# Attention takes its query tiles in the order middle, last, first, and the block's products stand ahead of the exponentials

## The reference

```python
h = tok(x)                       # gray, two 3x3 Scharr convolutions, (|dx| + |dy|) / 2: 256 rows of 256
h = concat([h, text(x_txt)])     # 128 rows of a low-rank embedding: 384 rows of 256 per image
h = h + attention(layernorm(h))  # 16 heads of 16, query i sees keys i-128 .. i
h = h + routed(layernorm(h))     # the 288 rows with the highest score get gelu(x @ w_block), the others x
h = h + ssm(layernorm(h))        # linear recurrence with a circulant matrix, done in the Fourier basis
h = h + moe(layernorm(h))        # shared FFN of 1024 plus two of eight experts, gated
```

## Time and profile before

| | us |
|---|---|
| median of three runs | 2317.09 (2313.73 to 2319.89) |
| profiled execution, its own time | 2323.64 |
| its span | 2321.8 |
| images 2 to 14, each, from one copy of `hc` to the next | 95.6 |
| image 0, with all loads | 158.6 |

### The profile page before, as it was taken

The page is one execution under the profiler, slowest core; times in us unless marked ns, Lnnn a source line. Parts: engine busy times, 40 slices in busy tenths (PEclk is TensorE's granted clock), DMA queues, the critical chain, the costliest instruction groups (busy, mean ns, idle before and its releaser), DMA issues.

```text
span 2321.8 us, 45095 instructions
## 1 busy us (share of the span) xinstructions
PE 2038.4 (88%) x13718; PEld 1599.1 (69%) x13812; DVE 1320.7 (57%) x3533; ACT 1111.4 (48%) x2541; POOL 796.0 (34%) x1535
## 2 busy tenths in 40 slices
PE   3778898898988989989899898987589999999997
PEld 1455666566665666666666566654489999999997
DVE  4536566565665666656566565664255555555554
ACT  0335445545455544554545545552155445655543
POOL 2213223232333323233322333233244544444454
PEclk9789999999999999999999999998789999999999
DMA  4210211202112021020220211201133223333222
GB/s 129 63 41 15 62 43 34 61 7 61 47 28 61 15 60 44 24 61 24 50 51 18 61 31 44 48 8 55 61 107 79 45 45 79 78 51 79 48 45 41
DMA packets 83556, 116.35 MB, mean 50 GB/s; under 512 B 23718, under 2 KB 63974, under 8 KB 81190
## 3 DMA queue, kind: packets, MB, share of 16 engines
q1 hardware_dynamic: 57414, 85.14, 13.7%
q0 software_dynamic: 23360, 27.91, 7.3%
q10 hardware_dynamic: 2736, 2.76, 0.4%
HBM read 51.58 MB, written 26.71 MB: 34 GB/s over the span
## 4 chain that ended last, share of the span: by engine, by line
PE 57%; issue 15%; DVE 13%; POOL 5%; ACT 4%; DMA 3%; SPq 1%; DVEq 1%; POOLq 0%; ACTq 0%
PE ps L1743 9%; PE ps L1598 6%; PE ps L1517 4%; PE ps L1463 3%; PE ps L1755 3%; PE ps L1756 3%; PE ps L1754 3%; PE ps L1585 3%; PE ps L1530 2%; PE ps L1508 2%; PE ps L1635 2%; DMA result<-yb,idx_o 2%; PE ps L1437 2%; PE ps L1485 2%; ACT prob L781 2%
## 5 line engine op out<-in xcount | busy, mean ns | idle before, releaser
L1092 DVE TENSOR_REDUCE mx<-ps 128x2 f32<-128x512 f32 (+1 forms) x384 | 227.8, 597 | 298.7 <-PE ps L1509 250.1
L781 ACT ACTIVATE prob<-ps,mx 128x256 f32<-128x256 f32 (+1 forms) x768 | 295.4, 445 | 165.5 <-DVE mx L1092 146.0
L773 ACT ACTIVATE pT<-ps 128x512 f32<-128x512 f32 (+1 forms) x384 | 204.0, 531 | 337.4 <-PE ps L1517 336.8
L883 ACT ACTIVATE hid_hi<-ps,b 128x256 fp32r<-128x256 f32 x408 | 204.5, 501 | 287.9 <-PE ps L1743 287.4
L1508 PE MATMUL ps<-ks,qs 96*128 96x512 f32 (+1 forms) x384 | 198.5, 522 | 71.6 <-issue 36.3
L1368 DVE TENSOR_TENSOR hid_lo<-hid_full,hid_hi 128x256 fp32r<-128x256 f32 x408 | 171.8, 426 | 151.8 <-ACT hid_full L886 140.6
L1517 PE MATMUL ps<-ident,prob 128*128 128x128 f32 x1280 | 211.4, 281 | 27.7 <-ACT prob L781 21.7
L1754 PE MATMUL ps<-w_hi,hid_hi 128*128 128x256 f32 x816 | 233.9, 287 | 0.0
L1755 PE MATMUL ps<-w_lo,hid_hi 128*128 128x256 f32 x816 | 229.6, 281 | 0.0
L1756 PE MATMUL ps<-w_hi,hid_lo 128*128 128x256 f32 x816 | 229.6, 281 | 0.0
L886 ACT ACTIVATE hid_full<-ps,b 128x256 f32<-128x256 f32 x408 | 205.1, 503 | 0.3 <-DVE hid_lo L1368 0.3
(11 more groups left out here) (256 smaller groups left out, 4311.6 us busy)
## 6 DMA issues: line engine op xcount, KB each, us to landing
w_raw<-in_w SPq DMA_DIRECT2D x16, 1024.0 KB, 6.0
xin<-in_x SPq DMA_DIRECT2D x32, 384.0 KB, 3.8
qs<-q_hi SPq DMA_DIRECT2D x128, 96.0 KB
ks<-k_hi SPq DMA_DIRECT2D x256, 48.0 KB
qs<-q_lo SPq DMA_DIRECT2D x64, 96.0 KB
ks<-k_lo SPq DMA_DIRECT2D x128, 48.0 KB
xn_rows<-xc SPq DMA_DIRECT2D x16, 384.0 KB, 2.5
result<-h SPq DMA_DIRECT2D x16, 384.0 KB, 2.5
```

Source lines behind the costliest of these rows:

```text
L781: ins = act.activation(prob[:, s % PB, hh, w], ps[:, s % 2, hh * 2 * P + w.start:(hh + 1) * 2 * P], ACT.Exp, bias=mx[:, s % 2, hh:hh + 1])
L883: act.activation(hid_hi[:, f], ps[:, f % 4, 0:CHUNK], ACT.Gelu_apprx_tanh, bias=b1[half][:, f:f + 1])
L1092: dve.tensor_reduce(mx[:, s % 2], sc, AX_X, ALU.max, negate=True).then_inc(max_done.sem, 1)
```

## The change

`ORDER = (1, 2, 0)`: units 0 to 7 are now those of the middle query tile, 8 to 15 of the last, 16 to 23 of the first, and each place that asked for the tile by the slot asks `ORDER`. The output projections move to slots `WO` = 16, 24, 31 (15, 23, 31 before). The slot constants move: the first `turn_chain` to slot 1; router scores and all three block tiles to slot 2, ahead of unit 2; on ScalarE the copies of `xcT` and `srow` and the block's Gelu to slot 0, ahead of the first exponential; rank counts to slots 1 to 3; `slot_ranks` to slot 1, now into PSUM bank 4, with a wait of TensorE for `cnt_ready` in slot 4; the sum over the values to slot 2; the `down` steps to slots 2, 3, 4, 5, 7, 8; text to 3 and 5; gray to 11; the second `turn_chain` to 12, the recurrence to 14, the edge steps to 15 to 18, `state_out` and `make_rows` to 19. The logits on VectorE move from slots 28 to 30 to slots 30 to 32, the `up` steps to slots 30 and 31 (one each) and behind the last slot (six). The value product no longer waits for the low part of the queries, and for its third tile waits for VectorE's last read of the keys' bank (`k_read`). No arithmetic is added or taken away.

```diff
@@ -42,17 +42,20 @@
 UPT = NH // HG
+ORDER = (1, 2, 0)
 PB, TB = 3, 3
...
 VW = 2 * DK
-
-RANKS, TURN0, BLOCK, RANK = 4, 2, 4, 6
-DOWN, TEXT, GRAY_AT, TURN1 = 8, 8, 13, 15
-STATE, CONV, OUT = 17, 18, 22
-ROWS, TURN2, UP = 22, 27, 28
-UPS = {29: (0, 1, 2), 31: (3,), 32: (4,)}
-UPS_LAST = (5, 6, 7)
+WO = [UPT * (i + 1) + PV + 4 + (i < NT - 1) for i in range(NT)]
+
+RANKS, TURN0, BLOCK, RANK = 1, 1, 2, 1
+TEXT, GRAY_AT, TURN1 = 3, 11, 12
+DOWNS = {2: 0, 3: 1, 4: 2, 5: 3, 7: 4, 8: 5}
+STATE, CONV, OUT = 14, 15, 19
+ROWS, TURN2, UP, LOGIT = 19, 27, 28, 30
+UPS = {30: (0,), 31: (1,)}
+UPS_LAST = (2, 3, 4, 5, 6, 7)
 NEWTON = 3
@@ -767,14 +771,14 @@
                     u = s - TURN
-                    k0 = 0 if u >= UPT else 1
+                    k0 = 0 if ORDER[u // UPT] else 1
                     act.wait_ge(turned.sem, turned.at(b, u + 1))
...
                 if s < NU:
-                    w = slice(0 if s >= UPT else P, 2 * P)
+                    w = slice(0 if ORDER[s // UPT] else P, 2 * P)
                     act.wait_ge(max_done.sem, max_done.at(b, s + 1))
@@ -835,17 +839,19 @@
                     if chain:
-                        if s in (TURN0, TURN1):
-                            turned_rows(b - 1, (TURN0, TURN1).index(s))
-                        if s in (BLOCK + 1, BLOCK + 2):
-                            block_outputs(b - 1, s - BLOCK - 1)
+                        if s == 0:
+                            turned_rows(b - 1, 0)
+                            block_outputs(b - 1, 0)
+                            block_outputs(b - 1, 1)
+                        if s == TURN1:
+                            turned_rows(b - 1, 1)
                     if att:
...
                         round_first()
-                    if head and s == TEXT - 1:
+                    if head and s == TEXT - 2:
                         text_rows(b + 1)
@@ -1062,8 +1068,9 @@
                 for m in range(KB):
-                    dve.scalar_tensor_tensor(out=k_lo[:, m], in0=ps[:, 2 + m, 0:T], scalar=bk[:, m:m + 1],
-                                             in1=k_hi[:, m], op0=ALU.add, op1=ALU.subtract)
+                    ins = dve.scalar_tensor_tensor(out=k_lo[:, m], in0=ps[:, 2 + m, 0:T], scalar=bk[:, m:m + 1],
+                                                   in1=k_hi[:, m], op0=ALU.add, op1=ALU.subtract)
+                ins.then_inc(k_read.sem, 1)
@@ -1103,11 +1110,11 @@
                     dve.tensor_tensor(cx[:], cx[:], sumv[:], ALU.add).then_inc(cx_ready.sem, 1)
-                if s >= UPT + PV + 5 and (s - UPT - PV - 5) % UPT == 0:
-                    i = (s - UPT - PV - 5) // UPT
+                if s - 1 in WO:
+                    i = WO.index(s - 1)
                     dve.wait_ge(wo_done.sem, wo_done.at(b, i + 1))
                     dve.wait_ge(hbo_ready.sem, hbo_ready.at(b, 1))
-                    dve.tensor_tensor(h1[:, i], hbo[:, i], ps[:, 5, D:2 * D], ALU.add).then_inc(h1_ready.sem, 1)
+                    dve.tensor_tensor(h1[:, ORDER[i]], hbo[:, ORDER[i]], ps[:, 5, D:2 * D], ALU.add).then_inc(h1_ready.sem, 1)
@@ -1199,7 +1206,7 @@
                     chain_scale(b, 2)
-                if s == UP:
+                if s == LOGIT:
@@ -1210,14 +1217,14 @@
                     link(ins, chain_step, b)
-                if s == UP + 1:
+                if s == LOGIT + 1:
                     dve.memset(spare[:], 0.0)
...
                     link(dve.tensor_copy(pick[:], i8[:, :, 0:2].rearrange("p i k -> p k i")), chain_step, b)
-                if s == UP + 2:
+                if s == LOGIT + 2:
                     link(dve.tensor_tensor(hot[:].rearrange("p k i e -> p (k i) e"),
@@ -1240,7 +1247,7 @@
                 link(dve.tensor_tensor(picked[:], hot[:].rearrange("p k i e -> p k (i e)"),
-                                       ps[:, 5, 0:NT * NE].unsqueeze(1).to_broadcast([P, 2, NT * NE]), ALU.mult),
+                                       ps[:, 4, 0:NT * NE].unsqueeze(1).to_broadcast([P, 2, NT * NE]), ALU.mult),
                      slot_step, b)
@@ -1277,7 +1284,7 @@
                         powers(2 ** (s - 2))
-                    if late and s == DOWN + 6:
+                    if late and s == max(DOWNS) + 1:
                         shared_sum(b - 2)
@@ -1478,8 +1485,9 @@
                 pe.wait_ge(ctx_ready.sem, ctx_ready.at(b, 0))
-                pe.wait_ge(parts_ready.sem, parts_ready.at(b, 1))
                 for i in range(NT):
+                    if i == 2:
+                        pe.wait_ge(k_read.sem, k_read.at(b, 1))
                     dst = ps[:, 4, i * D:(i + 1) * D] if i < 2 else ps[:, 3, 0:D]
@@ -1496,12 +1504,12 @@
                 if s < NU:
-                    i, g = s // UPT, s % UPT
+                    i, g = ORDER[s // UPT], s % UPT
                     c0 = 0 if i else P
...
                     m, r = g % KB, g // KB
-                    if i == 0 and m == 0:
+                    if s < UPT and m == 0:
                         pe.wait_ge(stacked[r].sem, stacked[r].at(b, stacked[r].per))
@@ -1513,15 +1521,15 @@
                     for hh in range(HG):
-                        for k in range(0 if u >= UPT else 1, 2):
+                        for k in range(0 if ORDER[u // UPT] else 1, 2):
                             ins = pe.transpose(ps[:, 2 + u % 2, (2 * hh + k) * P:(2 * hh + k + 1) * P],
...
                     u = s - PV
-                    i, g = u // UPT, u % UPT
+                    i, g = ORDER[u // UPT], u % UPT
                     if g == 1:
-                        pe.wait_ge(ctx_ready.sem, ctx_ready.at(b, i))
+                        pe.wait_ge(ctx_ready.sem, ctx_ready.at(b, u // UPT))
                     pe.wait_ge(pT_ready.sem, pT_ready.at(b, u + 1))
@@ -1544,8 +1552,8 @@
                     ins.then_inc(cx_turned.sem, 1)
-                if s >= UPT + PV + 4 and (s - UPT - PV - 4) % UPT == 0:
-                    i = (s - UPT - PV - 4) // UPT
+                if s in WO:
+                    i = WO.index(s)
                     pe.wait_ge(cxT_ready.sem, cxT_ready.at(b, i + 1))
@@ -1605,27 +1613,27 @@
                 if att:
-                    pe.wait_ge(sumv_ready.sem, sumv_ready.at(b + 2, 1))
+                    pe.wait_ge(v_ready.sem, v_ready.at(b + 2, 1))
                 flat_hot = hot2[:].rearrange("p i e -> p (i e)")
                 w = NT * NE
-                pe.matmul(ps[:, 5, 0:w], ltri[:], flat_hot, start=True, stop=False)
+                pe.matmul(ps[:, 4, 0:w], ltri[:], flat_hot, start=True, stop=False)
                 for i in range(1, NT):
-                    pe.matmul(ps[:, 5, i * NE:w], ones_bf[:], flat_hot[:, 0:w - i * NE], start=False, stop=False)
-                pe.matmul(ps[:, 5, 0:w].rearrange("p (i e) -> p i e", i=NT), ones_bf[:],
+                    pe.matmul(ps[:, 4, i * NE:w], ones_bf[:], flat_hot[:, 0:w - i * NE], start=False, stop=False)
+                pe.matmul(ps[:, 4, 0:w].rearrange("p (i e) -> p i e", i=NT), ones_bf[:],
                           cnt[:].unsqueeze(1).to_broadcast([P, NT, NE]), start=False, stop=True
...
             def chain(b, s, head):
-                if s in (TURN0, TURN1, TURN2):
+                if s in (TURN1, TURN2):
                     turn_chain(b, (TURN0, TURN1, TURN2).index(s), head)
...
                     for k in range(KB):
-                        pe.matmul(ps[:, 7, 0:T], wr_bc[:, k], xcT[:, k], start=(k == 0), stop=(k == KB - 1))
+                        ins = pe.matmul(ps[:, 7, 0:T], wr_bc[:, k], xcT[:, k], start=(k == 0), stop=(k == KB - 1))
+                    ins.then_inc(block_done.sem, 1)
                     block_tile(0)
-                    block_tile(1).then_inc(block_done.sem, 1)
-                if s == BLOCK + 2:
+                    block_tile(1)
                     pe.wait_ge(block_ready.sem, block_ready.at(b, 1))
@@ -1663,18 +1671,24 @@
                         values(b + 1)
+                    if att and s == BLOCK:
+                        values_sum(b)
+                    if late and s == BLOCK:
+                        down(b - 2, 0, chained, head)
+                    if late and s == PV + 1:
+                        pe.wait_ge(cnt_ready.sem, cnt_ready.at(b - 2, 1))
+                    if chained and s == TURN0:
+                        turn_chain(b - 1, 0, head)
                     if att:
                         unit(b, s)
-                    if att and s == 1:
-                        values_sum(b)
                     if late and s == RANKS:
...
                         text(b + 1)
-                    if late and DOWN <= s < DOWN + 6:
-                        down(b - 2, s - DOWN, chained, head)
+                    if late and s > BLOCK and s in DOWNS:
+                        down(b - 2, DOWNS[s], chained, head)
                     if head and CONV <= s < CONV + 4:
...
                     if chained and s == OUT:
```

(1 more changed line is left out.)

## The result

| | us |
|---|---|
| median of four runs after the change | 2228.89 (2226.42 to 2231.07) |
| the kernel before, four runs beside it | 2318.49 (2313.73 to 2322.36) |
| ratio | 0.9614, 95% interval 0.9591 to 0.9637 |
| profiled execution after, its own time and its span | 2226.72 and 2224.9 |
| images 2 to 14, mean, from one copy of `hc` to the next | 89.8 (95.6 before) |

What follows compares the result with a forecast made beforehand. TensorE, busy 88%, bounds the kernel through its waits. Minus 67.6 us for images 2 to 14 and minus 7 elsewhere take 2323.6 to 2249.0; less 6.5 for the runs' median, 2242.5 us, range 2212 to 2284.

Steps and rivals of the forecast that it cites:

- What bounds the kernel, and the work itself: Whole image: TensorE's work without the slow clock about 85.3 us; its waits go from 8.9 to 5.1.
- Front: Slots 0 to 2: two of four table loads go, four waits become 0.3 us, minus 4.1 an image.
- The clock: TensorE's slow stretch beside the 2.52 us wait: with that wait gone, 0.9 us an image is taken back.
- Middle: Slots 3 to 14: nothing waits, and the 1.57 us wait before the second `turn_chain` goes.
- Last tile: Slots 16 to 26: half-size units cover handoffs less; waits of 4.3 us, the largest 1.75; plus 2.3 an image.
- End: Last residual to the next `turn_chain`: 0.55 us open where 0.88 was, minus 0.3 an image.
- Images 0, 1 and 15, and behind: Three images outside 2 to 14: minus 3 us each; pass behind the last image: plus 2; together minus 7.
- The series of the last tile: Rival: from slot 20 each unit takes a full round, 11.2 us more per image, 2388 in all; chance 0.06.
- Half the gain goes back: Rival: five waits each 0.5 us longer, or the clock falls there; images of 92 to 94, 2263 to 2289; chance 0.17.
- Near TensorE's work alone: Rival: the last tile costs less than counted; images of 87 to 88.5 us, time 2198 to 2218; chance 0.13.
- The table load: ScalarE's table switches: 1.28 us per load, with no drain in the trace where the skill gives another 1.38.

Runs made afterwards that it cites:

- the natural order: The changed kernel with the query tiles in the order first, middle, last, all slots as changed: 2217.58 us, ratio 0.9562.
- the order-alone kernel: The kernel before with the tile order middle, last, first and nothing else changed: 2399.75 us, ratio 1.0336.

## Why the prediction was right

*What bounds the kernel, and the work itself.* Right. TensorE's work without the slow clock was put at 85.3 us per image. In image 5 of the changed kernel the listed waits are 0.21, 0.42, 0.24, 1.68, 0.27, 0.69 and 0.55, together 4.1, and 89.3 less that is 85.2. So the whole question was the sum of the waits: 5.1 forecast, 4.1 there, and 0.5 of clock in the mean. That makes 89.8 where 90.4 was forecast, 8 us in thirteen images.

*Front.* Right. Two loads per image are left, slot 2 starts 9.1 us behind `turn_chain` (8.75 forecast) without a wait, and 0.43 is open, for `xcT`, where 0.3 was forecast. One part undone alone, the Gelu, gives 2.9 back.

*The clock.* Right in sign, incomplete as a term. Taking back 0.9 for the stretch at 747 to 752 was fair: the kernel before without any fall measured 1.4 less. What failed is the silence on the other side. The sum had a wait of 1.75 in the tail and no clock behind it; only a rival had it. It does fall there, in eight of thirteen images, for 0.6 to 0.9 each. The reason given against it, that the steps behind the wait of 1.25 at 803.70 keep their length, did not carry over to a wait of 1.68.

*Middle.* Right in all its covers: no wait in slots 2 to 8 (one of 0.24 comes at 719.29), the second `turn_chain` 31.2 behind the first (31.0) with no wait, the stacking in time. One cover was overrated. The last halo transfer issues late:

```profile
726.59 0.59 SPq L452 DMA_DIRECT2D halo<-gray  x1
```

With 1.7 to land, counted from the start of the issue as the kernel with the first tile in the middle shows, it is in at 728.3, and the edge step starts at 729.2: 0.9 of margin. The prediction had 1.9, and 2.6 if it is counted the same way. The first of the six issues at 34.4 behind `turn_chain`, where `gray` was to end at 33.0. That is why the order with the first tile in the middle met it.

*Last tile.* Right in its place and its largest term (1.68, forecast 1.75) and its last (0.55, forecast 0.55). The second `pT` copy costs 0.69 (0.75). Two terms were too large: `xn` costs 0.27 and not 0.75, because the score tile and transposes ahead of it cover more, and the 0.5 before the `cx` turns is not there at all. 3.2 instead of 4.3.

*End.* 0.20 for 0.55: the `up` steps now cover all of the statistics, and the `turn_chain` waits for its bank (`hid`), no longer for `xc`.

*Images 0, 1 and 15, and behind.* Here the terms of 3 were mis-sized: in the profiled pair images 0 and 15 gained 8.4 and 8.6 more than forecast, which is past the bound of 5, and each as much as the whole loop did (8.1). For image 0 the profile misled, and the explanation isn't the change. Its first edge step takes 2.90 in both, the length at the lower clock; how many of the others do is not the same. Before:

```profile
35.54 2.93 PE L1437 MATMUL ps<-gray,band 128*128 128x256 f32 x6
...
39.55 2.93 PE L1437 MATMUL ps<-gray,band 128*128 128x256 f32 x6
...
43.33 1.56 PE L1437 MATMUL ps<-gray,band 128*128 128x256 f32 x6
```

After:

```profile
34.40 1.56 PE L1444 MATMUL ps<-gray,band 128*128 128x256 f32 x6
```

The kernel before with idle products, whose image 0 is that of before word for word, also has 1.56 there, and its copy of `hc` comes at 149.25 where before has 158.57. Against that, the changed kernel's 147.15 is 2.1 better; 3 was forecast. So most of the 11.4 is the clock at the start and not the change. That would also fit the profiled execution's 6.5 above its median, and the 10 us over which the runs of before spread; only profiled executions show it, so that stays a reading. The forecast's reason for the 3, the half-size units, shows as 0.5 against the natural order (147.65), in one profile of each. Over the kernels of this study the copy comes at 144.7 to 159.8.

Image 15 gained 10.1 from one `turn_chain` to the next: listed waits went from 14.3 to 9.0, and TensorE's busy time for the same products from 73.6 to 69.0, as the clock went from 0.90 to 0.98:

```profile
1408.32:1486.47 78.15, 69.00 (x472) 48.86 (x473) 47.33 (x138) 41.73 (x94) 25.36 (x58) 0.98 0.15 48
```

The prediction had read 0.90 in the row and made no term of it. Image 1 gained 5.4, as the loop did.

Behind the last image the pass is 7.4 longer where 2 was forecast. 2.1 are ahead of its `turn_chain`: seven `up` steps now stand there. 2.6 lie from there to the first scatter, 10.5 instead of the 7.9 of the earlier trace rows. 1.6 of them are what the forecast had in mind: VectorE starts the slot computation 6.8 behind `turn_chain`, behind the counts (5.2 before). The other cause, 1.06, it didn't have; it is in ScalarE's rows of after:

```profile
1492.40 0.81 ACT L812 ACTIVATE g<-ps 128x768 f32<-128x768 f32 x1 [2.10 <-PE ps L1584]
1493.23 1.28 ACT L827 ACT_TABLE_LOAD   x1
1494.53 0.21 ACT L827 ACTIVATE gates<-gates 128x3 f32<-128x3 f32 x1
...
1494.84 0.17 DVE L1256 TENSOR_SCALAR gates<-gates 128x3 f32<-128x3 f32 x1 [1.06 <-ACT gates L827]
```

The Gelu now comes ahead of the gates' exponential, so its table load lies on the path to the scatter, and VectorE waits for `gates`; before, it stood ahead of `srow` at 1590.38, beside TensorE's work. The ordering that saves two loads in an image puts one on the path here. The other 2.7 lie later in the pass. These are readings of rows; no run took the 7.4 apart.

*The rivals.* The series of the last tile did not come: each unit waits for the exponential two before, and only one wait passes a microsecond. "Half the gain goes back" named a mechanism that is there, the clock behind the tail's waits, and took it for 1.6 to 3.6 us an image where 0.5 came. "Near TensorE's work alone" was about as near in time as the forecast: 2228.9 lies between its upper end, 2218, and 2242.5. By the image it was not: 89.8 is in the forecast's 89 to 92 and above the rival's 88.5. What the total gained beyond the loop comes from images 0 and 15, a good part of it clock that the forecast had no term for, less the 5.4 lost behind the last image. That these partly cancel is luck.

*The table load.* The Trainium skill ("ScalarE: Activation LUTs", what a load costs) gives 1.38 us of drain with each switch. After the change too, the load starts at 696.00, where the Gelu ends (695.17 and 0.81), and the exponential at 697.29, where the load ends: no drain shows on either side, and the measured 1.28 a load is what counts.

## What to carry to other kernels

Undo each part of a change by itself. This one bundled a schedule that brings the whole gain with an order of the tiles that costs 0.8 us an image. Price a wait of TensorE by what stands behind it too. In this kernel waits of 1.7 to 2.5 us in a stretch otherwise busy cost another 0.5 to 1.5 us an image through the clock, and products that compute nothing, put into the gap, are a cheap way to measure that share. When a wait is removed, ask what is next: `cx` took over from the exponential at full size, VectorE's read from the halo rows at a third. And read the clock of each stretch before its waits are summed; it was 0.90 in the one image whose gain was most underrated.

## What was not expected of the hardware

The granted clock isn't a function of one wait. Behind the same wait of 1.68 it falls in images 3, 4, 7, 8, 10, 11, 13 and 14 and stays at 1.00 in the others. Where one gap was filled (the 2.52 of before), it fell behind another (0.87 and 1.31) which had left it at 1.00 until then, and the kernel gained 0.3% instead of the 0.8% that images without a fall would give (1.4 of 95.6, thirteen times). And with waits almost unchanged it fell two or three times in an image of the order-alone kernel, where nine idle products gave 4.3 us back. The Trainium skill ("TensorE: Matmul & The Clock Gate", part 1) ties the lower clock to idleness of the array; the rows agree that it falls behind idleness, but which of several like gaps it takes is left open by them.
